# Gated attention of a 12-part decoder: a loop over four groups becomes 21 straight-line slots

## The reference, cut to what matters

```python
def _L3_attn_ref(x, Wv, bv, Wg, bg, Win, bin_, Wout, bout, g_qq, b_qq, ...):
    v = silu(xc @ Wv + bv)          # 256 -> 512
    gate = silu(xc @ Wg + bg)       # 256 -> 512
    x_ = silu(xc @ Win + bin_)      # 256 -> 128
    quad_q, quad_k = x_ * g_qq + b_qq, x_ * g_qk + b_qk
    lin_q, lin_k = x_ * g_lq + b_lq, x_ * g_lk + b_lk
    attn = einsum(quad_q, quad_k) / sqrt(512), causal inside the group
    attn = square(relu(attn))
    kv = cumsum(lin_k^T v over the groups) - kv
    o = (attn @ v + lin_q @ kv) * gate
    return o @ Wout + bout          # 512 -> 256
```

## Time and profile before

| | |
|---|---|
| median of 3 runs | 3279.15 us (3278.52 to 3281.96) |
| profiled execution | 3280.81 us, its span 3278.7 us |
| busy, share of the span | TensorE 82%, weight load 56%, Vector 56%, Scalar 37%, POOL 24% |
| mean granted TensorE clock | 0.904 of 2.4 GHz |
| gated attention | about 2388 to 2582 us of the span |

### The profile page before, as it was taken

One profiled execution on the slowest core, in us unless ns is written; L12 is line 12 of the kernel. 1 busy time (PEld: TensorE's weight loads), 2 busy tenths in 40 slices (PEclk: granted clock), 3 DMA queues, 4 the chain that ended last, 5 costly groups with the idle time before them and its releaser, 6 DMA issues. The chain is left out here.

```text
span 3278.7 us, 47320 instructions
## 1 busy us (share of the span) xinstructions
PE 2688.4 (82%) x15122; PEld 1841.3 (56%) x15123; DVE 1828.0 (56%) x3976; ACT 1209.4 (37%) x3052; POOL 793.0 (24%) x613
## 2 busy tenths in 40 slices
PE   3998977779777779599998979869867688879996
PEld 1565754457545446377776757546534466436664
DVE  6875963359787634344444559843343488433334
ACT  2323642236577513244343436511111366312211
POOL 4433520035200034122222236421100143131110
PEclk8999988899877779799999999879977798889998
DMA  9001000000200223200001020131110300321012
GB/s 290 1 1 44 12 17 0 0 14 1 56 4 4 36 86 111 84 1 1 1 1 46 11 65 1 66 133 31 39 51 0 78 14 1 139 105 32 31 32 96
DMA packets 158950, 142.27 MB, mean 43 GB/s; under 512 B 59012, under 2 KB 146068, under 8 KB 158388
## 3 DMA queue, kind: packets, MB, share of 16 engines
q1 hardware_dynamic: 145828, 111.95, 11.8%
q0 software_dynamic: 8688, 23.82, 2.0%
q10 hardware_dynamic: 4256, 4.20, 0.4%
HBM read 97.12 MB, written 42.81 MB: 43 GB/s over the span
## 5 line engine op out<-in xcount | busy, mean ns | idle before, releaser
L873 POOL TENSOR_TENSOR room<-room 128x1024 f32<-128x1024 f32 x144 | 273.3, 1898 | 454.2 <-DVE room L818 453.3
L812 DVE TENSOR_REDUCE room<-room 128x8 f32<-128x1024 f32 x144 | 174.0, 1208 | 0.0
L1312 PE MATMUL l3f_hidden<-room,Y 128*128 x312 | 146.1, 612 | 5.3 <-DVE Y L1552 4.9
L1331 PE MATMUL l3f_out<-room,Y 128*128 x624 | 141.1, 379 | 1.6 <-DVE Y L1577 1.6
L549 PE MATMUL l2a_proj<-room 128*128 128x256 f32 x512 | 128.7, 400 | 14.3 <-ACT room L896 14.3
L1331 PEld LDWEIGHTS l3f_out<-room,Y 128*128 128x128 f32 x624 | 118.5, 190 | 34.1 <-issue 20.0
L873 POOL TENSOR_TENSOR room<-room,l2a_rinv 128x1024 f32<-128x1024 f32 x32 | 60.7, 1897 | 253.4 <-DVE l2a_rinv L818 253.4
L549 PEld LDWEIGHTS l2a_proj<-room 128*128 128x128 f32 x512 | 97.3, 197 | 32.2 <-issue 17.0
L1688 POOL DMA_INDIRECT results<-Y,l3f_dest x39 | 37.5, 961 | 300.4 <-DVE Y L1585 165.3
L942 ACT ACTIVATE room<-l2a_scores,l2a_nmx 128x128 f32<-128x128 f32 x256 | 72.3, 381 | 93.6 <-DVE l2a_nmx L804 93.6
L2244 POOL DMA_INDIRECT sorted_rows<-room,l1f_place_i x32 | 31.6, 986 | 305.3 <-DVE l1f_place_i L1999 296.1
(11 more groups left out here) (740 smaller groups left out, 6829.6 us busy)
## 6 DMA issues: line engine op xcount, KB each, us to landing
sorted_rows<-zeros SPq DMA_DIRECT2D x1, 16512.0 KB, 67.5
room<-in_L_ffn_w SPq DMA_DIRECT2D x16, 1024.0 KB, 11.6
room<-in_L_ffn_W SPq DMA_DIRECT2D x16, 1024.0 KB, 12.0
Y<-sorted_rows SPq DMA_DIRECT2D x62, 129.0 KB, 2.1
room<-in_ctx SPq DMA_DIRECT2D x24, 256.0 KB, 2.7
room<-results SPq DMA_DIRECT2D x12, 512.0 KB, 7.4
room<-sorted_rows SPq DMA_DIRECT2D x39, 129.0 KB, 2.1
Y<-results SPq DMA_DIRECT2D x8, 512.0 KB, 5.9
```

The source lines that it names most:

```text
L812: dve.tensor_reduce(rsum[:, u % 2, :], p[:, u % (TURN + 1), :, :], AX.X, ALU.add)
L873: pool.tensor_tensor(p[:, u % (TURN + 1), :, :], p[:, u % (TURN + 1), :, :], rinv[:, u % (TURN + 1), :].unsqueeze(2).to_broadcast([P, HEAD ...
L1312: mm = pe.matmul(hbank[a][:, :], rowsT[:, par, kc, :], chip.room[:, bass.ds(at + (kc * F + a * half_f), half_f)], start=(kc == 0), stop=(k ...
L1331: mm = pe.matmul(obank[par][:, 0:D], hT[:, f, :], chip.room[:, bass.ds(at + (SLOT // 2 + f * D), D)], start=(f == 0), stop=(f == HC - 1))
```

## The change

The loop is written out as 21 slots, k from -2 to 18. `yT` and `aT` get a second buffer, and each kind of result has a PSUM bank and semaphores of its own; the counters start at zero, without the loop's lead. In slot k TensorE turns o of tile k-3, makes v of tile k, projects the output of tile k-3, attends tile k-2 and makes the gate of tile k. The slots of a group g, counted by r = (k+2) mod 4, then end with a step for it: r = 0 turn its rows, r = 1 features, r = 2 scores; Vector squares at r = 3. Tile 4g is made in slot 4g, which has r = 2. Vector now also runs bn_aggr per tile and, at the end, the variance, square root (with Scalar) and reciprocal; the next block starts without them. The cut diff (removed lines are those of the kernel above; "..." marks what is left out):

```diff
         yn = sb("yn", [P, GR, D])
-        yT = sb("yT", [P, KC, TG])
+        yT = sb("yT", [P, 2, KC, TG])
...
-        aT = sb("aT", [P, GR, P])
+        aT = sb("aT", [P, 2, GR, P])
         o = sb("o", [P, 2, INNER])
         oT = sb("oT", [P, OC, P])
         bank = [chip.ps(f"gau_bank{i}", scope) for i in range(8)]
+        y_bank, x_bank, far_bank, near_bank = bank[0:2], bank[0], bank[0], bank[1]
+        o_bank, v_bank, gate_bank, oT_bank, out_bank = bank[2:4], bank[4], bank[5], bank[6], bank[7]
...
+        end = {n: sem(f"end_{n}") for n in ("var_ready", "std_ready")}
...
+        SLOTS = range(-2, NB + 3)
...
     @block.tensor
     def _(pe):
...
         w.wait(pe)
...
+
+        def turn_rows(g):
+            pe.wait_ge(yn_ready, g + 1)
+            if g:
+                pe.wait_ge(aT_ready, g)
             for kc in range(KC):
...
                 for j in range(GR):
...
+                    mm = pe.transpose(y_bank[kc][:, j * P:(j + 1) * P], yn[:, j, kc * P:(kc + 1) * P], chip.ident[:, :])
                 mm.then_inc(turned[kc], 1)
+
+        def features(g):
             for kc in range(KC):
...
+                pe.wait_ge(yT_ready[kc], g + 1)
             for kc in range(KC):
...
+                mm = pe.matmul(x_bank[:, :], w.v["x"][:, kc, :], yT[:, g % 2, kc, :], start=(kc == 0), stop=(kc == KC - 1))
             mm.then_inc(x_filled, 1)
...
+
+        def scores(g):
+            pe.wait_ge(feats_ready, g + 1)
             qq, qk, lq, lk = feats
             for j in range(GR):
...
+                pe.matmul(near_bank[:, j * P:(j + 1) * P], qk[:, j * P:(j + 1) * P], qq[:, j * P:(j + 1) * P], start=True, stop=True)
             for j in range(GR):
...
+                mm = pe.matmul(far_bank[0:CH, j * CH:(j + 1) * CH], lk[:, j * P:j * P + CH], lq[:, j * P + CH:(j + 1) * P], start=True, stop=True)
             mm.then_inc(scores_ready, 1)
...
+
+        def project(n, to, name):
+            g, j = divmod(n, GR)
+            for kc in range(KC):
+                mm = pe.matmul(to[:, :], yT[:, g % 2, kc, j * P:(j + 1) * P], w.v[name][:, kc, :], start=(kc == 0), stop=(kc == KC - 1))
+            return mm
+
+        def make_v(n):
+            if n:
+                pe.wait_ge(v_biased, n)
+            project(n, v_bank, "v").then_inc(v_filled, 1)
+
+        def make_gate(n):
+            if n:
+                pe.wait_ge(gate_biased, n)
+            project(n, gate_bank, "g").then_inc(gate_filled, 1)
+
+        def attend(n):
+            g, j = divmod(n, GR)
+            pe.wait_ge(aT_ready, g + 1)
+            pe.wait_ge(v_ready, n + 1)
+            if n >= 2:
+                pe.wait_ge(o_ready, n - 1)
+            pe.matmul(o_bank[n % 2][:, :], aT[:, g % 2, j, :], v[:, j, :], start=True, stop=True).then_inc(o_filled, 1)
+
+        def turn_o(n):
+            pe.wait_ge(o_ready, n + 1)
+            if n:
+                pe.wait_ge(oT_ready, n)
+            for c in range(OC):
+                mm = pe.transpose(oT_bank[:, c * P:(c + 1) * P], o[:, n % 2, c * P:(c + 1) * P], chip.ident[:, :])
+            mm.then_inc(oT_filled, 1)
+
+        def output(n):
+            pe.wait_ge(oT_ready, n + 1)
+            if n:
+                pe.wait_ge(y_added, n)
+            for c in range(OC):
+                mm = pe.matmul(out_bank[:, 0:D], oT[:, c, :], w.v["o"][:, c, :], start=(c == 0), stop=(c == OC - 1))
+            mm.then_inc(y_filled, 1)
+
+        for k in SLOTS:
+            g, r = divmod(k + 2, GR)
+            if 0 <= k - 3 < NB:
+                turn_o(k - 3)
+            if 0 <= k < NB:
+                make_v(k)
+            if 0 <= k - 3 < NB:
+                output(k - 3)
+            if 0 <= k - 2 < NB:
+                attend(k - 2)
+            if 0 <= k < NB:
+                make_gate(k)
+            if g < NG and r == 0:
+                turn_rows(g)
+            if g < NG and r == 1:
+                features(g)
+            if g < NG and r == 2:
+                scores(g)
 
     @block.vector
     def _(dve):
...
         dve.tensor_copy(within[:, :], chip.upper[:, :])
         dve.drain()
         dve.memset(within[0:CH, CH:P], 0.0)
         ln_stats_vector(chip, dve, chip.X, s, have=have_stats)
...
+
+        def normalise(g):
+            if g:
+                dve.wait_ge(turned[1], g)
             for j in range(GR):
                 b = g * GR + j
...
+                op = dve.tensor_scalar(yn[:, j, :], chip.X[:, b, :], chip.mv[:, b, 0:1], chip.rstd[:, b:b + 1], ALU.subtract, ALU.mult)
             op.then_inc(yn_ready, 1)
...
+
+        def empty_yT(g):
+            dve.wait_ge(turned[0], g + 1)
+            if g >= 2:
+                dve.wait_ge(gate_filled, GR * (g - 1))
+            dve.tensor_copy(yT[:, g % 2, 0, :], y_bank[0][:, :]).then_inc(yT_ready[0], 1)
+
+        def make_feats(g):
+            dve.wait_ge(xs_ready, g + 1)
             for f, mul, add in zip(feats, w.v["mul"], w.v["add"]):
                 op = dve.tensor_scalar(f[:, :], xs[:, :], mul, add, ALU.mult, ALU.add)
             op.then_inc(feats_ready, 1)
...
+
+        def square(g):
+            dve.wait_ge(scores_ready, g + 1)
+            dve.tensor_scalar(pos[:, :, :], near_bank[:, :].rearrange("p (j q) -> p j q", j=GR), INNER ** -0.5, 0.0, ALU.mult, ALU.max)
+            dve.drain()
+            if g >= 2:
+                dve.wait_ge(o_filled, GR * (g - 1))
+            dve.tensor_tensor(aT[:, g % 2, :, :], pos[:, :, :], within[:, :].unsqueeze(1).to_broadcast([P, GR, P]), ALU.mult)
+            dve.drain()
+            dve.tensor_tensor(aT[:, g % 2, :, :], aT[:, g % 2, :, :], pos[:, :, :], ALU.mult)
+            dve.drain()
+            dve.tensor_copy(aT[0:CH, g % 2, :, CH:P], far_bank[0:CH, 0:GR * CH].rearrange("p (j q) -> p j q", j=GR)).then_inc(aT_ready, 1)
+
+        def bias_v(n):
+            dve.wait_ge(v_filled, n + 1)
+            if n >= GR:
+                dve.wait_ge(o_filled, n - GR + 1)
+            dve.tensor_tensor(v[:, n % GR, :], v_bank[:, :], w.v["bv"], ALU.add).then_inc(v_biased, 1)
+
+        def bias_gate(n):
+            dve.wait_ge(gate_filled, n + 1)
+            dve.tensor_tensor(gate[:, n % GR, :], gate_bank[:, :], w.v["bg"], ALU.add).then_inc(gate_biased, 1)
+
+        def multiply(n):
+            dve.wait_ge(o_filled, n + 1)
+            dve.wait_ge(gate_ready, n + 1)
+            if n >= 2:
+                dve.wait_ge(oT_filled, n - 1)
+            dve.tensor_tensor(o[:, n % 2, :], o_bank[n % 2][:, :], gate[:, n % GR, :], ALU.mult).then_inc(o_ready, 1)
+
+        def add(b):
+            dve.wait_ge(y_filled, b + 1)
+            if b % GR == 0:
+                dve.wait_ge(bias_added, b // GR + 1)
+            dve.tensor_tensor(chip.X[:, b, :], chip.X[:, b, :], out_bank[:, 0:D], ALU.add).then_inc(y_added, 1)
+
+        def sums(b):
+            dve.drain()
+            dve.bn_stats(chip.bn[:, b, :], chip.X[:, b, :])
+            dve.drain()
+            dve.bn_aggr(chip.mv[:, b, :], chip.bn[:, b, :])
+
+        normalise(0)
+        w.wait(dve)
+        for k in SLOTS:
+            g, r = divmod(k + 2, GR)
+            if g < NG and r == 2:
+                make_feats(g)
+            if g < NG and r == 3:
+                square(g)
+            if 0 <= k < NB:
+                bias_v(k)
+            if 0 <= k - 3 < NB:
+                add(k - 3)
+            if 0 <= k - 2 < NB:
+                multiply(k - 2)
+            if 0 <= k - 3 < NB:
+                sums(k - 3)
+            if 0 <= k < NB:
+                bias_gate(k)
+            if g < NG and r == 0:
+                empty_yT(g)
+                if g + 1 < NG:
+                    normalise(g + 1)
+        dve.drain()
+        ln_stats_vector(chip, dve, chip.X, end, have="mv")
 
     @block.gpsimd
     def _(pool):
...
     @block.scalar
     def _(act):
...
         ln_stats_scalar(chip, act, s, have=have_stats)
         w.wait(act)
         act.preload_act_table(ACT.Silu)
...
+
+        def empty_yT(g):
+            act.wait_ge(turned[1], g + 1)
+            if g >= 2:
+                act.wait_ge(gate_filled, GR * (g - 1))
+            act.copy(yT[:, g % 2, 1, :], y_bank[1][:, :]).then_inc(yT_ready[1], 1)
+
+        def make_xs(g):
+            act.wait_ge(x_filled, g + 1)
+            if g:
+                act.wait_ge(feats_ready, g)
+            act.activation(xs[:, :], x_bank[:, :], ACT.Silu, bias=w.v["bx"]).then_inc(xs_ready, 1)
+
+        def empty_oT(n):
+            act.wait_ge(oT_filled, n + 1)
+            if n:
+                act.wait_ge(y_filled, n)
+            act.copy(oT[:, :, :], oT_bank[:, :].rearrange("p (c q) -> p c q", c=OC)).then_inc(oT_ready, 1)
+
+        def silu_v(n):
+            act.wait_ge(v_biased, n + 1)
+            act.activation(v[:, n % GR, :], v[:, n % GR, :], ACT.Silu).then_inc(v_ready, 1)
+
+        def silu_gate(n):
+            act.wait_ge(gate_biased, n + 1)
+            act.activation(gate[:, n % GR, :], gate[:, n % GR, :], ACT.Silu).then_inc(gate_ready, 1)
+
```

(59 more changed lines are left out.)

76 lines of the change are left out of this document (7 added, 69 removed).

## The result

The changed kernel took 3218.89 us in the median of four runs (3218.18 to 3222.84), the kernel before 3278.84 us beside it (3277.57 to 3281.96): a ratio of 0.9818 with a 95% interval of 0.9801 to 0.9835, so 60 us less, by the interval 54 to 65. The forecast was 3227 in a range of 3221 to 3241.

The account below looks back on a forecast made before the run. No engine was full; TensorE, nearest, was interrupted by waits and a lowered clock. 56.1 us saved less 1.3 for statistics gave 54.8, less 3 of allowances 52: 3227 us against the median, range 3221 to 3241.

Parts of the forecast that it names:

- The bound and the mechanism: Gated attention: TensorE nearest to full but interrupted; interleaved slots of 6.47 us at full clock, 30.0 per four with waits extra.
- the tail: Last three slots, with no v or gate to hide under: 13.5 us, the last add starting 0.2 later.
- the statistics: End of the gated attention: layer norm's final statistics moved in, 1.3 us on the end path.
- The allowances: Gated attention: tail clock 2 us, operand changes 1, code fetch 0, POOL's adds 0; 54.8 less 3 gives 52 saved.
- operand changes: TensorE's output instructions in the stage: between 0 and 13 x 0.1 us extra, taken as 1.
- at most 1: Gain side in the gated attention: the loop's register steps vanish, at most 1 us.
- What lies outside the stage is nought: Next block: dropping its statistics gains nothing, its first matmul awaiting the mask's DMA; up to 2 us if that came at once.
- The range: Whole kernel: own range 3221 to 3234 us, reaching on to 3241 through the late-slot and Vector cases.
- Scalar or Vector late in every slot: Steady slots: a wait of 0.7 us in 13 slots, 9 us less saved, 3236; at twice that 3245; chance 0.17.
- Vector the bound: Gated attention: Vector's operations at 1.5 times their spacing, 11 us, 3238; chance 0.06.
- Clock low: Whole stage: TensorE's clock stays at 1.2 GHz, 118 us more against 54 saved, 3343; chance 0.02.
- No interleaving: Slots serialised by a semaphore wait: iteration near today's 45 us, time within a few us of before; chance 0.03.

Follow-up runs that it names:

- run 5: Changed kernel with 122 drains added to Vector's program at the start of l3x; ratio 0.9837 (0.9819 to 0.9854) against the kernel before.
- Runs 2 and 3: Kernel before with six, then two, drains added to Vector's program at the start of l3x; ratios 0.998 and 0.9968 against the kernel before.
- two padded copies of the changed kernel: Changed kernel with two, and with 122, drains added to Vector's program at the start of l3x; ratios 0.9829 and 0.9837 against the kernel before.

## Why the prediction was right and where it was wrong

**The bound and the mechanism: right.** TensorE's own work at the full clock was the new length. Slot 6.49 us against 6.47, group 30.10 against 30.1, the tail from its first transpose to the last add 14.05 against 13.7, the work 129.82 against 130.96, the statistics 1.06 against 1.3. In run 5 the work is 131.3, so the sum lies between what two profiles of the same order show.

**The allowances: the first step that failed.** The forecast put the tail between 0 and 8.2 us and took 2 for its clock; the gaps of 0.7 to 1.5 us left that at the full level, so 0. "I take 1" for operand changes: eight output instructions stand (1.89 - 0.38)/7 = 0.216 us apart in most slots, so 0 there. The 0.23 of the earlier trace rows is left only behind the waits of the tail (1.99 for eight), and is most of the 0.35 us by which the tail is longer than its sum. On the gain side "at most 1" was left out of the sum: 0.62 came in the opening, where Vector's first instruction no longer follows seven semaphore increments (0.11 us behind the barrier instead of 0.76). The three were worth 3.6 us; two of them shrank 54.8 to 52. The work itself was 1.1 us shorter than summed, because the clock had risen by the first v in this profile: v and gate of tile 0 took 3.43 us, not the 4.7 that the sum has (3.44 and 1.24 for the old opening's clock). That was luck, since three of six kernels did not have it.

**"What lies outside the stage is nought": the second.** The sum ended at the stage's border. The last block gave 3.8 us more, for a delay that the profile of before did show: 19 waits of TensorE for Vector in that block's loop, 4.9 us, which I had not asked to explain. Runs 2 and 3 show that more Vector code ahead of the loop can remove these waits. Why the change did, and what in the place of the code decides, stays open; that it came out as a gain and not as a loss was luck.

**The range: the third.** It held the unknown prices but not the scatter of the rest. One profile of before was taken for the kernel: its gated attention was 4 us longer than in each of four later ones (work 187.12 against 182.9 to 183.4), and untouched blocks move by 4 to 11 us between profiles. Against the later profiles the stage saves some 53 us, with the last block 57, and that lies inside the measured interval of 54 to 65. That the remaining 3 us are chance is argued from the scatter, not shown. The two padded copies of the changed kernel, whose last blocks are as short (459.35 and 459.95), bear it out: their ratios of 0.9829 and 0.9837 are 56 and 53 us of 3279. Measured like them, the change would have come out inside the range. The 52 of the forecast also has luck in it: the profile that it started from had 4 us more in the stage than the later ones, and from one of those the same sum would have given about 48.

**The rivals.** Scalar or Vector late in every slot: no, the output starts behind v without a wait in the steady slots. Vector the bound: no, 58.58 of 99 us busy; the Trainium skill's flush after each operation (VectorE: DVE Perf Modes, The DRAIN you can't avoid) does not come on top of the rows' durations here, as the forecast had read from the 0.77 us spacing. Clock low: no, 1.00. No interleaving: no.

**Which part carried it.** From 183 us of work: straight code 2 to 3, the overlap of tiles 42 (180.24 to 138.11), the group's steps ahead 6.8, and 1.5 that the opening's clock gave by chance, to 129.82. Each of these is from one profile.

## What to carry to other kernels

Where one engine has most of the work and waits in short pieces, price the new stage as that engine's spacings at the full clock, once through the order; this gave 130.96 us where 129.82 and 131.3 were measured. Put the scatter of everything untouched into the range, best from more than one profile, and do not subtract an allowance for each unknown from the likeliest value. After an edit that changes the length of any engine's code, look at the loops behind it before the edit is credited or blamed.

## What was not expected of the hardware

A block with a hardware loop over 39 tiles, two in each turn, took 463.2 us or 459.4 to 459.9 depending on two or six more drains in Vector's program before the loop. The way back of Vector's loop had three lengths in all (0.39, 0.53 and 0.62 us, the same within 0.01 in every turn after the first few), and the same place modulo 128 instructions had the longest in one kernel (463.29) and the shortest in another (459.95). The Trainium skill (Runtime: NRT & Kernel Launch, Instruction fetch mechanics) says that a taken branch outside the fetched window forces a fetch by DMA before execution can go on; here no instruction packet moves during that loop, so this rule does not explain the 0.23 us per turn. Behind idle 128x512 matmuls (4.2 us in the profile) the opening ran at the full clock. The same wait of 3.0 us was followed by the half clock in one profile of the same code and by the full clock in another. Untouched blocks took 209.6 to 220.6 us (routed experts) from one profile to the next.
